# Loading the first four adjacency row tiles in two column halves, with x between them (graph layer and routed FFN, one core)

## The reference

```
def _L0_gnn_ref(x, adj, W1, b1, W3, b3, Wf, bf):
    h = jax.nn.relu(adj @ (x @ W1) + b1)
    h = jax.nn.relu(adj @ (h @ W3) + b3)
    return jnp.tanh(h @ Wf + bf)
...
x = x + _L0_gnn_ref(_layernorm(x, axis=-1), adj, ...)
x = x + _L0_ffn_ref(_layernorm(x, axis=-1)[None], ...)[0]
```

## Time and profile before

| what | value |
|---|---|
| median of three runs | 667.63 us (667.21 to 668.91) |
| profiled execution, own time | 671.28 us |
| its span | 669.2 us |
| PE busy | 612.0 us, 91% |
| DVE, ACT, POOL busy | 341.6, 312.5, 147.5 us |
| mean granted clock of PE | 0.983 |
| DMA | 63.74 MB, mean 95 GB/s |

### The profile page before, as it was taken

How to read it: one execution, slowest core, us unless ns; L and a number is a source line. 1 busy time by engine, 2 the same in 40 slices (tenths; PEclk the granted TensorE clock), 3 DMA queues, 4 the chain that set the end, 5 groups by cost and what they waited for, 6 DMA issues and landing times.

```text
span 669.2 us, 11466 instructions
## 1 busy us (share of the span) xinstructions
PE 612.0 (91%) x3472; PEld 519.8 (78%) x3473; DVE 341.6 (51%) x752; ACT 312.5 (47%) x589; POOL 147.5 (22%) x143
## 2 busy tenths in 40 slices
PE   1999999999999988989888999999999999999970
PEld 1888888887867676768767898888888888888860
DVE  3786434465646676636644333337333636377620
ACT  1567565766455465446522223335333536356520
POOL 3000000000000505027444123322332233223222
PEclk9999999999999999999989999999999999999985
DMA  8995000020002673521163022117111715376312
GB/s 303 359 333 203 5 1 1 0 95 1 1 3 92 123 177 119 159 64 41 17 194 90 10 33 34 29 21 219 32 28 19 219 32 147 88 211 166 80 29 32
DMA packets 34739, 63.74 MB, mean 95 GB/s; under 512 B 4954, under 2 KB 27100, under 8 KB 32636
## 3 DMA queue, kind: packets, MB, share of 16 engines
q1 hardware_dynamic: 26044, 52.32, 23.9%
q0 software_dynamic: 8224, 10.53, 9.7%
q10 hardware_dynamic: 432, 0.39, 0.2%
HBM read 54.02 MB, written 10.26 MB: 96 GB/s over the span
## 4 chain that ended last, share of the span: by engine, by line
PE 81%; DVE 4%; issue 4%; ACT 4%; DMA 3%; POOL 1%; SPq 0%; POOLq 0%; ACTq 0%; DVEq 0%
PE bank L1551 40%; PE bank L1420 8%; PE bank L1422 8%; PE bank L1421 8%; PE bank L1396 4%; PE bank L1598 4%; PE bank L1447 3%; DMA adj_s<-in_adj 2%; PE bank L1433 2%; PE bank L1384 2%; PE bank L1544 1%; DVE ring L915 1%; PE bank L1471 1%; POOL slot_rows L479 1%; PE bank L1445 1%
## 5 line engine op out<-in xcount | busy, mean ns | idle before, releaser
L1551 PE MATMUL bank<-ew,xeT 128*128 128x512 f32 x840 | 202.2, 395 | 4.6 <-DVE ew L1246 2.6
L1551 PEld LDWEIGHTS bank<-ew,xeT 128*128 128x128 f32 x840 | 154.7, 188 | 36.3 <-issue 4.2
L915 DVE TENSOR_TENSOR ring<-adj_s,ring 128x512 fp32r<-128x512 f32 x128 | 87.6, 689 | 76.5 <-ACT adj_s L596 40.8
L1551 PE MATMUL bank<-ew,heT 128*128 128x256 f32 x840 | 112.0, 291 | 4.7 <-issue 2.4
L1420 PE MATMUL bank<-ring,Z 128*128 128x512 f32 x256 | 110.1, 430 | 6.3 <-DVE ring L915 4.7
L1551 PEld LDWEIGHTS bank<-ew,heT 128*128 128x128 f32 x840 | 105.5, 196 | 6.2 <-issue 6.1
L1422 PE MATMUL bank<-ring,Z 128*128 128x512 f32 x256 | 100.6, 393 | 0.0
L1421 PE MATMUL bank<-ring,Z 128*128 128x512 f32 x256 | 100.2, 391 | 0.0
L512 POOL DMA_INDIRECT out<-y_st,idx_st x29 | 45.5, 1569 | 191.0 <-ACT y_st L748 169.0
L479 POOL DMA_INDIRECT slot_rows<-val,route x32 | 35.9, 1122 | 224.1 <-issue 222.4
L754 ACT ACTIVATE sil<-bank 128x512 f32<-128x512 f32 x58 | 34.6, 596 | 86.3 <-PE bank L1551 86.3
(11 more groups left out here) (183 smaller groups left out, 620.4 us busy)
## 6 DMA issues: line engine op xcount, KB each, us to landing
w_raw<-in_L_ffn_W SPq DMA_DIRECT2D x24, 1024.0 KB
adj_s<-in_adj SPq DMA_DIRECT2D x16, 1024.0 KB, 6.7
x_in<-in_x SPq DMA_DIRECT2D x4, 512.0 KB, 5.3
x_res<-in_x SPq DMA_DIRECT2D x4, 512.0 KB, 3.6
out<-x SPq DMA_DIRECT2D x4, 512.0 KB, 3.9
ffn_in_rows<-x_res SPq DMA_DIRECT2D x4, 512.0 KB
xg<-ffn_in_rows,idx POOLq DMA_INDIRECT x39
Wg<-in_L_gnn_W SPq DMA_DIRECT2D x2, 256.0 KB, 3.8
```

The source lines that it names most:

```text
L915: nc.vector.tensor_tensor(lo, src, hi, ALU.subtract).then_inc(s_lo, 1)
L1551: last = nc.tensor.matmul(out_ap, stat[:, sl, k, :], w_at(k, wl), start=(k == k0 and sl == wl == 0), stop=(k == k1 - 1 and sl == 1))
```

## The change

For the first four row tiles, SP issues the left halves (columns 0 to 1023) of all four, without a wait between them, then x_load(1), then the right halves (each once its left half has landed), then x_load(2). Each of these tiles has a semaphore of its own, `s_adj0[t]`. Tiles 4 to 15 follow as before; x_load(3) stands ahead of tile 5. `transpose_block` waits for the four left halves at block 0 and for the right ones at block 8. DVE's first part of x_norm for group 1 moves from ahead of z1_lo(0) to behind lo_of_block(0).

```
+        s_adj0 = [sem(f"s_adj_row{t}") for t in range(CT)]
...
-            for t in range(NT):
-                if t >= 2:
-                    sp.wait_ge(s_adj[t % 2], 16 * (t // 2))
-                if CT <= t < CT + NC - 1:
-                    x_load(t - CT + 1)
+            for half in range(2):
+                cols = slice(half * N // 2, (half + 1) * N // 2)
+                for t in range(CT):
+                    if half == 1:
+                        sp.wait_ge(s_adj0[t], 16)
+                    sp.dma_start(adj_s[:, t, cols], adj_rows[t, :, cols]).then_inc(s_adj0[t], 16)
+                x_load(half + 1)
+
+            for t in range(CT, NT):
+                if t < CT + 2:
+                    sp.wait_ge(s_adj0[t - CT], 32)
+                else:
+                    sp.wait_ge(s_adj[t % 2], 16 * ((t - CT) // 2))
+                if t == CT + 1:
+                    x_load(3)
...
             x_T_lo(0)
             x_T_lo(1)
-            x_norm(1, 0)
             z1_lo(0)
...
                 lo_of_block(s)
+                if s == 0:
+                    x_norm(1, 0)
...
             def transpose_block(s):
                 c, jb = s // NT, s % NT
-                if jb == 0:
+                if c == 0 and jb % (NT // 2) == 0:
+                    for t in range(CT):
+                        pe.wait_ge(s_adj0[t], 16 * (jb // (NT // 2) + 1))
+                if c >= 1 and jb == 0:
                     for par in range(2):
-                        pe.wait_ge(s_adj[par], 16 * (CT * (c + 1) // 2))
+                        pe.wait_ge(s_adj[par], 16 * (CT * c // 2))
```

## The result

The changed kernel's median was 665.12 us over 6 runs, that of before 668.76 over 6 (667.63 in the three shown ahead of the prediction). The ratio is 0.994, 95% interval 0.9922 to 0.9957: 4.0 us less, 2.9 to 5.2. Forecast were 662.4 us and 5.2 us less, range 660.7 to 664.6. So the kernel became faster, by less than forecast, and its time lay 0.5 us above the range.

What follows compares the result with a forecast made beforehand. PE's 5.0 us wait for whole adjacency tiles was taken to bound the start. Removing 4.97 us of idle PE and 0.2 through earlier fast pace, with other terms 0, gave -5.2 us: 662.4 us, range 660.7 to 664.6.

Steps and rivals of the forecast that it cites:

- The bound: At the start, PE waits 5.0 us at L1396 for four whole adjacency tiles; an earlier start comes off the end.
- DVE's times: Early DVE work: lo_of_block(0) begins at 15.3 us and group 1 of x is needed at 15.9.
- The moved norm: x_norm(1, 0) behind lo_of_block(0) on DVE: costs nothing beyond what it hides under, 0.79 us if its cover were gone.
- rival D: Smaller transfers run slowly, so the halves land at 20.3 us, later than whole tiles today: 670.0 us, chance 0.02.
- the landing of the left halves: First adjacency loads: 2816 KB up to the last left half, so landing at about 11.4 us, bounds 11.1 to 13.7.
- The 1.5 us of cover: Slack at the first transposes: halves landed before PE finishes z1_rows(0) at 12.99 us.
- rival A: Group 1 of x lands late, at 18.8 us, and delays DVE: gain 2.3, 665.3 us; includes late halves; chance 0.11.
- what PE's pace does: PE's fast pace could come by some 15.4 us, before z1_rows(1), saving PE 0.8 us, mostly held back by DVE.
- The 0.2 us of the sum: The part of PE's earlier fast pace counted as gain in the forecast: 0.2 us.
- 4.97: PE's idle time removed at the start: first transposes at 12.99 instead of 17.96, 4.97 us.
- the base: Time of the kernel before from which the gain was subtracted: the median of the runs, 667.63 us.
- Rival B: PE's lower-clock stretch, as at 345 to 350 us, is added (664.1) or lost (660.7): chances 0.06 and 0.05.

Runs made afterwards that it cites:

- norm_only: Kernel before with only x_norm(1, 0) moved behind lo_of_block(0), its loads unchanged; ratio 1.0009 to the kernel before.
- halves_only: Changed kernel with DVE's order of before, x_norm(1, 0) ahead of z1_lo(0); ratio 0.9949 to the kernel before.
- hold_all: Changed kernel with group 1 of x and all right halves issued only after the four left halves landed; ratio 0.9957 to the kernel before.
- hold_right: Changed kernel with only the right halves held until all left halves landed, x's group 1 directly behind the left ones; ratio 0.9949 to before.
- x_last: Changed kernel with groups 1 and 2 of x issued behind the four right halves; ratio 1.0045 to the kernel before.
- halves_w1: Changed kernel with DVE's split of W1 moved behind the scaling of the first rows of x; ratio 0.9941 to the kernel before.

## Why the prediction was right or wrong

**Right.** The bound: PE's wait at L1396 was on the path, and what was taken from it reached the end. SP's x_res issue, which follows PE's and DVE's work, came at 134.80 instead of 139.81 in the first pair, so 5.0 of the 5.17 us were still there, and at 136.04 instead of 139.21 in the second, 3.2 of 3.4. DVE's times, lo_of_block(0) at 15.3 and x_norm asked for at 15.9, were met to 0.1 us. DVE didn't hold PE back, though: from 13 to 24 us PE waited for nothing in the changed kernel but, in its second execution, the left half, so PE's own pace set the third product. The moved norm was free (norm_only, halves_only). PE had no idle time from 25 to 66 and waited for no right half at block 8. Halving was no loss, and rival D's 670 us didn't come.

**Wrong: the landing of the left halves.** "2816 KB. That is exactly what stands before the end of the second whole tile today", so "the halves should land at about 11.4". Equal bytes were taken for equal time, and the number and size of the transfers was put at nothing. Two transfers of 1 MB landed at 11.4 to 11.7; four of 512 KB at 12.9 to 13.9 in the seven executions with the same four left halves (changed kernel 12.96 and 13.70, hold_all 13.56, hold_right 13.77, x_last 13.88, halves_only 13.24 and halves_w1 12.86). The number of transfers, and with it the size of each, is the cause as far as it was tested; rows of 4 KB, and what was queued behind, are not. The 1.5 us of cover were mostly none.

One reading in support was wrong: x didn't move at 324 to 512 GB/s up to 5 us but up to 4.5, and from there to 5.4 the row shows 174, 0 and 82, so the engines did empty between transfers, even with two of 1 MB issued. The queue, too, held not 1.5 but 2.5 MB at these waits, counting the half waited for; nothing hung on it.

The rule of the Trainium skill that was weighed there ("DMA: Bandwidth & Descriptors", section Bandwidth: large transfers) had the direction right, and I set it to nothing; the estimate of a start after 20 us, from that page's figure for 64 KB, is not what the runs show. The case stood in the prediction as "the halves land at 13.7 (gain 4.3)", inside rival A with 0.11; it is the usual one.

**Wrong: what PE's pace does.** "it could come by some 15.4, before z1_rows(1)". In the six executions of the changed order of loads with W1's split in its place (changed kernel twice, halves_only, hold_all, hold_right, x_last) z1_rows(1) still ran at the slow pace or mostly so (1.22 to 1.28 us), and the four transposes after it took 0.44 in one of them, 0.59 and 0.75 in two, and 0.85, the slow pace, in three. The 0.2 us of the sum weren't there in most of them, and the spread of the third product follows the pace as much as the landing.

The size: third products at 27.58 and 27.01 before, 22.41 and 23.61 after, and 27.51 and 23.22 in norm_only and halves_only, whose loads are those of before and after. The means differ by 27.37 - 23.08 = 4.3 us. The first transposes of the same six are at 17.96, 17.83 and 16.96 and at 13.08, 13.81 and 13.36: 17.58 - 13.42 = 4.2 us, where the sum had 4.97. Half of what is missing is the late landing (13.42 for 12.99), and half is that 17.96 was the latest of the three starts of before. The three ratios give 4.0, 3.9 and 3.4. So the mechanism was right, and its term of 4.97 + 0.2 was too large by about 1.

**Wrong: the base.** The 662.4 us stood on a median of 667.63 from three runs. Later sets of before gave 668.3 to 668.8 (6 to 31 runs each, single ones from 666.2 to 673.2). This 1.1 us is the other half of the miss in the absolute time: 665.1 - 662.4 = 2.7 = 1.1 (base) + 1.2 (gain 4.0 instead of 5.2) + 0.4 (two medians don't differ exactly by the ratio). Either of the two alone would have left the time inside the range (663.5 or 663.6 us).

**Rival A**, x late, didn't come, since group 1 was there by 14.6 in halves_only and by 15.9 in the changed kernel. Its price was too mild for a kernel in which it does: with x behind the right halves (x_last) it wasn't 665.3 but 671.65 us, because group 1 landed at 22.05, later than the 18.8 of the rival, and because the pause took PE back to the lower clock. It was the rival that could have ended on the other side.

**Rival B**'s slow stretch at 340 to 350 us was in the first execution of either kernel and in neither second one. As far as these four show, it belongs to an execution and not to the change.

**Open.** Why four transfers end so unevenly; and why the lower clock comes near 340 to 350 us in one execution of a kernel and not in the next, and why it comes before PE's last matmuls are done in some and not in others, which no kernel here isolates.

## What to carry to other kernels

To bring a first block forward, load only the columns that it needs, try it in one transfer, or in pieces small enough to land with room to spare, and see to it that the next stage's own input (here x) stands directly behind it and not behind the rest. A landing time read for some bytes in two transfers doesn't hold for the same bytes in four: here it was 0.7 to 2.5 us later, more than the cover of 1.5 us in most executions. Judge a gain of a few us by several profiled executions of both kernels, since one pair showed 5.2 us where the ratio gave 4.0, and compare executions with the same mean granted clock.

## What the hardware showed unexpectedly

- The same 2 MB, with nothing behind them, landed at 11.67 in two transfers, 11.96 in one, 13.03 and 13.56 in four. Four transfers to 64 partitions each took until 15.05.
- The granted clock read 1.00 at 18 to 22 us while matmuls ran at half pace (0.43 us for 512 columns up to 23.16 in norm_only). The trace's first record of a granted clock comes where the durations change (22.0 in before, 23.0 in norm_only, 16.4 in the changed kernel), and ahead of it the rows read 1.00; the first rise is to be read from durations. In the first 30 us only x_last, after its pause, read 0.50.
- 1.0 us of earlier transposes (norm_only against before) gave 0.1 us at the third product, since the fast pace came later in that execution.
- The same 24 last matmuls of the same kernel took 4.62 us in one execution and 3.12 in another. Two such stretches, 1.7 and 1.5 us, are most of the 3.8 us between the two spans of before.
